# Block-selective-scan kernel: column tiles on TensorE, more states summed by DMA, skip, shift and bias by DMA, twelve product buffers, a written timetable

## The reference

```
mod = silu(c) @ wmod                                  # six rows of 512 for each sequence: sa ca ga sb cb gb
h   = layernorm(x) * (1 + ca) + sa
xs, z = split(h @ w_in.T + b_in);  z = silu(z)
dt  = softplus(xs @ w_dt.T + b_dt)
B, C = xs @ w_B.T + b_B, xs @ w_C.T + b_C             # 16 states
for each token:  state = exp(A * dt) * state + dt * B * xs;   y = sum over the 16 states of state * C
y   = ((y + D * xs) * z) @ w_out.T + b_out
x   = x + ga * (layernorm(y + h) * gamma + beta)
h   = layernorm(x) * (1 + cb) + sb
s   = h @ Win + bin                                   # 64 columns
g   = sum over 16 units of relu(s * W1 + b1) * W2 + b2
x   = x + gb * (g @ Wout + bout)
```

## Time and profile before

| | |
|---|---|
| runs | 4577.39, 4574.64, 4576.27 us |
| profiled execution | 4574.68 us |
| its span | 4572.9 us |
| granted TensorE clock, mean | 0.990 |
| busy: PE, ACT, DVE, POOL | 95%, 83%, 81%, 79% |
| DMA | 388.89 MB, mean 85 GB/s |

### The profile page before, as it was taken

One profiled execution on the slowest core, in us unless ns is written; L12 is line 12 of the kernel. 1 busy time (PEld: TensorE's weight loads), 2 busy tenths in 40 slices (PEclk: granted clock), 3 DMA queues, 4 the chain that ended last, 5 costly groups with the idle time before them and its releaser, 6 DMA issues. The chain is left out here.

```text
span 4572.9 us, 69933 instructions
## 1 busy us (share of the span) xinstructions
PE 4356.8 (95%) x22528; PEld 2784.8 (61%) x22528; DVE 3698.9 (81%) x5132; ACT 3814.2 (83%) x6371; POOL 3596.2 (79%) x1999
## 2 busy tenths in 40 slices
PE   7999999999999999999999999999999999999997
PEld 3666666666666666666666666666666666666664
DVE  3778888888888888888888888888888888888885
ACT  3788888888888888888888888888888888888885
POOL 3787878887878877877878878878788878788784
PEclk8999999999999999999999999999999999999999
DMA  4233233333233333332333333332333333333322
GB/s 138 73 79 87 81 89 82 85 81 88 80 94 81 83 88 87 85 87 77 86 93 83 89 82 84 83 90 78 91 76 89 87 86 86 86 77 89 86 77 58
DMA packets 177763, 388.89 MB, mean 85 GB/s; under 512 B 22693, under 2 KB 22693, under 8 KB 177402
## 3 DMA queue, kind: packets, MB, share of 16 engines
q1 hardware_dynamic: 140538, 250.19, 17.4%
q0 software_dynamic: 36864, 134.23, 15.3%
HBM read 215.50 MB, written 34.63 MB: 55 GB/s over the span
## 5 line engine op out<-in xcount | busy, mean ns | idle before, releaser
L379 POOL TENSOR_TENSOR work<-work,c_bc 128x1024 f32<-128x1024 f32 x1024 | 2463.3, 2418 | 765.9 <-DVE work L1140 676.7
L1140 DVE TENSOR_TENSOR_SCAN work<-work,state,b_ps 128x512 f32<-128x512 f32 x1792 | 2257.7, 1274 | 301.1 <-PE b_ps L468 272.7
L852 ACT ACTIVATE work<-u_td,b_td 128x512 f32<-128x512 f32 x2048 | 1453.2, 710 | 163.7 <-PE b_ps L468 158.3
L842 ACT ACTIVATE work<-dt_t,neg_a 128x512 f32<-128x512 f32 x2048 | 1451.3, 709 | 4.7 <-DVE work L1140 4.4
L468 PE MATMUL b_ps<-ident,work 128*128 128x128 f32 x8192 | 1253.3, 276 | 65.0 <-DVE work L1140 57.1
L468 PEld LDWEIGHTS b_ps<-ident,work 128*128 128x128 f32 x8192 | 974.8, 142 | 505.3 <-issue 303.2
L543 PEld LDWEIGHTS y_ps<-ident,work 128*128 128x128 f32 x6144 | 740.0, 142 | 481.7 <-issue 466.0
L543 PE MATMUL y_ps<-ident,work 128*128 128x128 f32 x6144 | 862.8, 273 | 1.6 <-DMA work<-work 1.3
L692 PE MATMUL dense<-h_t,w_in_t 128*128 128x512 f32 x1024 | 514.5, 599 | 1.1 <-DVE u_td L1223 1.1
L600 PE MATMUL dense<-w_out_t,proj 128*128 128x512 f32 x1024 | 509.9, 595 | 0.0
L658 PE MATMUL dense<-xs_t,w_dt_t 128*128 128x512 f32 x1024 | 501.2, 593 | 0.0
(11 more groups left out here) (115 smaller groups left out, 4530.4 us busy)
## 6 DMA issues: line engine op xcount, KB each, us to landing
c_bc<-c_d SPq DMA_DIRECT2D x512, 256.0 KB, 3.3
work<-work POOLq DMA_DIRECT2D x256, 512.0 KB, 5.6
xn<-in_x SPq DMA_DIRECT2D x128, 256.0 KB, 5.1
x<-in_x SPq DMA_DIRECT2D x128, 256.0 KB, 4.3
out_dram<-x SPq DMA_DIRECT2D x128, 256.0 KB, 4.4
work<-in_wmod SPq DMA_DIRECT2D x2, 1024.0 KB, 6.5
w_in_t<-in_w_in_t SPq DMA_DIRECT2D x2, 1024.0 KB, 9.9
gain_shift<-par_d SPq DMA_DIRECT2D x8, 256.0 KB, 6.0
```

What stands on the lines that cost most here:

```text
L379: gp.tensor_tensor(made_here, both(hs, HS_RING, s * U + i), c_bc[:, (s * N + n) % C_RING:(s * N + n) % C_RING + 1, :].to_broadcast([P, 2, ...
L842: A(decay[:, (s * U + i) % DEC_RING, :], dt_t[:, s % 2, j, :], ACT.Exp, scale=neg_a[:, j, n:n + 1]).then_inc(S["dec_done"], 1)
L852: A(v[:, n % V_RING, tb, :], u_td[:, tb, :], ACT.Copy, scale=b_td[:, s % 2, tb, n:n + 1]).then_inc(S["v_done"], 1)
L1140: V.tensor_tensor_scan(hs[:, (s * U + i) % HS_RING, :], decay[:, (s * U + i) % DEC_RING, :], b_ps[:, i % 2, :], state[:, i:i + 1] if s % N ...
```

## The change

- PE: `g` is computed in two column tiles of 64 weight columns, each with its own half of the 512 tokens (`tile_position`); `cb` in four column tiles of 32, each with 128 tokens; `turn_b` is a single transpose; `out` uses 64 rows of the array instead of 128, and its bias row is gone.
- HELD has six states: 0, 1 and 3, 4 are chains of three products (n, n + 1, n + 2), 6 and 8 begin pairs. 40 units are left for PE. A sum in a chain waits, at POOL, for the sum before it.
- The skip is a DMA from `xs_t` onto the products of state 3, the shift two DMAs of 512 KB onto `x1`, and the bias `gb * bout` one DMA of 1 MB onto `x1`; each source row of shift and bias is spread from DRAM. The POOL additions for them are gone.
- The sums are issued one product or more after the one that they wait for, in slots of their own (`sum`).
- Twelve `pr` buffers instead of ten.
- Each part has a slot written in a table (PE_AT, AT), for all engines.

```diff
--- before.py
+++ after.py
@@ -19,48 +19,75 @@
-    V_RING, DEC_RING, HS_RING, PR_RING, C_RING = 2, 6, 6, 10, 3
-    LAG = 4
-
-    HELD = (0, 6, 8, 11)
-    SUM_LAG = 3
+    V_RING, DEC_RING, HS_RING, PR_RING, C_RING = 2, 6, 6, 12, 3
+
+    HELD = (0, 1, 3, 4, 6, 8)
...
-    SKIP_AT = (8, 10)
+    SKIP_IN = 3
...
+    PE_AT = {}
+    for entry in """g.0@0 g.1@0 g.2@0 g.3@0 g.4@1 g.5@2 g.6@2 yz.0@2 g.7@3 res.0@3 yz.1@3 pre.0.0@4 yz.2@4 pre.0.1@5
...
+    AT = dict(
+        xsh=(13, 17),
+        x1=(17, 17, 19, 19),
+        bout=55,
...
+        y=(14, 14, 18, 24, 28, 28, 34, 34, 36, 37, 40, 40, 45, 46, 46, 46, 46, 46, 46, 47, 47, 51, 52, 52, 54, 54, 55, 56, 57, 61, 61, 61, 62, 62, 62, 62, 62, 64, 64, 64),
+        sum=(6, 8, 9, 11, 13, 17, 17, 20, 21, 25, 30, 32, 39, 40),
+    )
...
@@ -69,24 +96,16 @@
-    def add_slot(r):
-
-        return r + LAG + SUM_LAG * summed(r // KD) - (r in (U - 4, U - 2, U - 1)) - (r == U - 1)
-
-    ADDS = sorted((r for r in range(U) if r // KD not in HELD), key=lambda r: (add_slot(r), r))
+    SUM_AT = [i for i in range(0, U, 2) if summed(i // KD) or i // KD == SKIP_IN]
+
+    ADDS = [r for r in range(U) if r // KD not in HELD]
 
     def added(r):
 
         return ADDS.index(r) + 1
 
     def slot(*part):
...
+            def store_c(f):
+                yield AT["c_store"]
+                sp.wait_ge(S["cb_done"], at("cb_done", f, 1))
+                sp.wait_ge(S["prod_done"], at("prod_done", f - 2, U // 2))
+                for tb in range(TB):
+                    sp.dma_start(c_d[f % 2][:, tb * P:(tb + 1) * P], cb_t[tb * 2 * N:tb * 2 * N + N, :]
+                                 ).then_inc(S["c_stored"], Q)
...
@@ -379,30 +411,55 @@
                 gp.tensor_tensor(made_here, both(hs, HS_RING, s * U + i),
                                  c_bc[:, (s * N + n) % C_RING:(s * N + n) % C_RING + 1, :].to_broadcast([P, 2, T]), ALU.mult
                                  ).then_inc(S["prod_done"], 1)
-                if i in SKIP_AT:
-                    gp.wait_ge(S["prod_done"], at("prod_done", s, i // 2 + 1))
-                    gp.wait_ge(S["skip_done"], at("skip_done", s, j + 2))
-                    gp.tensor_tensor(made_here, made_here, xs_t[:, j:j + 2, :], ALU.add).then_inc(S["skip_added"], 1)
 
             def add_products(s, i):
 
                 gp.wait_ge(S["prod_done"], at("prod_done", s, i // 2 + 1))
+                if i // KD - 1 == SKIP_IN:
+                    gp.wait_ge(skip_added[i % KD // 2], (s + 1) * Q)
+                if s * SUMS + sums(i - KD):
+                    gp.wait_ge(sum_done[i % KD // 2], s * SUMS + Q * sums(i - KD))
                 gp.dma_start(both(pr, PR_RING, s * U + i), both(pr, PR_RING, s * U + i - KD), accum_op=ALU.add
                              ).then_inc(sum_done[i % KD // 2], Q)
 
+            def add_skip(s, i):
+                j = i % KD
+                gp.wait_ge(S["prod_done"], at("prod_done", s, i // 2 + 1))
+                gp.wait_ge(S["skip_done"], at("skip_done", s, j + 2))
+                gp.dma_start(both(pr, PR_RING, s * U + i), xs_t[:, j:j + 2, :], accum_op=ALU.add
+                             ).then_inc(skip_added[j // 2], Q)
+
+            def sum_up(s):
+                for i, first in zip(SUM_AT, AT["sum"]):
+                    yield first
+                    if i // KD == SKIP_IN:
+                        add_skip(s, i)
+                    if summed(i // KD):
+                        add_products(s, i)
+
+            def shifted(b):
+                for n in range(TB // 2):
+                    yield AT["xsh"][n]
+                    gp.wait_ge(S["par_stored"], 4 * Q)
+                    for tb in (2 * n, 2 * n + 1):
+                        gp.wait_ge(xb_loaded[tb], (b + 1) * Q)
+                    gp.dma_start(x1[:, 2 * n:2 * n + 2, :], par_d[1:2, b // NC:b // NC + 1, :].to_broadcast([P, 2, D]),
+                                 accum_op=ALU.add).then_inc(xsh_done[n], Q)
+
             def attended(b):
                 for tb in range(TB):
-                    yield made("out", tb) + 6
-                    if tb == 0:
-                        gp.wait_ge(S["gs_loaded"], (b // NC + 1) * 2 * Q)
-                    gp.wait_ge(xb_loaded[tb], (b + 1) * Q)
-                    gp.tensor_tensor(x1[:, tb, :], x1[:, tb, :], gs[:, 1, :], ALU.add
-                                     ).then_inc(S["xsh_done"], 1)
-                    yield made("pre", tb, 3) + 3
-                    gp.wait_ge(S["xsh_done"], at("xsh_done", b, tb + 1))
+                    yield AT["x1"][tb]
+                    gp.wait_ge(xsh_done[tb // 2], (b + 1) * Q)
                     gp.wait_ge(S["t2_done"], at("t2_done", b, tb + 1))
                     gp.tensor_tensor(x1[:, tb, :], x1[:, tb, :], tmp[:, tb, :], ALU.add
                                      ).then_inc(S["x1_done"], 1)
+
+            def add_bout(b):
+                yield AT["bout"]
+                gp.wait_ge(S["par_stored"], 4 * Q)
+                gp.wait_ge(S["xn2_done"], at("xn2_done", b, TB))
+                gp.dma_start(x1[:, :, :], par_d[3:4, b // NC:b // NC + 1, :].to_broadcast([P, TB, D]),
+                             accum_op=ALU.add).then_inc(S["bout_added"], Q)
 
             def gate_out(g):
                 yield 38
...
@@ -410,13 +467,16 @@
                 gp.wait_ge(S["late_loaded"], N_LATE * Q)
                 gp.tensor_tensor(wout_g[:, :], wout_g[:, :], wout_b[:, :], ALU.mult).then_inc(S["wout_done"], 1)
 
-            def step_size(f, b):
+            def step_size(f):
...
@@ -537,20 +595,35 @@
                 if summed(i // KD):
                     pe.wait_ge(sum_done[j // 2], s * SUMS + Q * sums(i))
                 pe.wait_ge(S["prod_done"], at("prod_done", s, i // 2 + 1))
-                if i - j % 2 in SKIP_AT:
-                    pe.wait_ge(S["skip_added"], at("skip_added", s, j // 2 + 1))
+                if i // KD == SKIP_IN:
+                    pe.wait_ge(skip_added[j // 2], (s + 1) * Q)
                 for tb in range(TB):
                     last = mm(y_ps[:, tb, j * P:(j + 1) * P], pr[:, (s * U + i) % PR_RING, tb * P:(tb + 1) * P],
                               ident[:, :], is_transpose=True, start=(i == ADDS[0]), stop=(i == ADDS[-1]))
                 last.then_inc(S["y_added"], 1)
+
+            def units(s):
+                for r, first in zip(ADDS, AT["y"]):
+                    if first < U:
+                        yield first
+                        add_unit(s, r)
+
+            def late_units(b):
+                for r, first in zip(ADDS, AT["y"]):
+                    if first >= U:
+                        yield first - U
+                        add_unit(b, r)
 
             def add_g(s, c, k):
                 if k == 0:
                     pe.wait_ge(S["w2dg_done"], 1)
                     pe.wait_ge(S["s_copied"], at("s_copied", c, 1))
                 pe.wait_ge(S["rel_done"], at("rel_done", c, k + 1))
-                mm(long(s, "g")[:, :], w2_dg[:, k, :], tmp[:, k % RELU_RING, :], start=(k == 0), stop=(k == J - 1)
-                   ).then_inc(S["g_used"], 1)
+                for h in range(2):
+                    last = mm(long(s, "g")[h * M:(h + 1) * M, 0:T // 2], w2_dg[:, k, :],
+                              tmp[:, k % RELU_RING, h * (T // 2):(h + 1) * (T // 2)], start=(k == 0), stop=(k == J - 1),
+                              tile_position=(0, h * M))
+                last.then_inc(S["g_used"], 1)
 
             def turn_y(s, b, c, j):
                 to = inside(s, "g" if j == 0 else "pre.0")
@@ -576,7 +649,9 @@
                 else:
                     pe.wait_ge(S["t1_done"], at("t1_done", b, (tb + 1) // 2))
                     pe.wait_ge(S["out_done"], at("out_done", c, tb - 1))
-                mm(to[:, :], gm[:, tb * P:(tb + 1) * P], wout_g[:, :], start=True, stop=True).then_inc(S["out_ps"], 1)
+                h = tb // 2
+                mm(to[:, :], gm[h * M:(h + 1) * M, tb % 2 * P:(tb % 2 + 1) * P], wout_g[h * M:(h + 1) * M, :], start=True,
+                   stop=True, tile_position=(h * M, 0)).then_inc(S["out_ps"], 1)
 
             def add_residual(s, b, c, tb):
                 to = long(s, "pre", tb)
@@ -663,16 +738,16 @@
             def add_cb(s, f, k):
                 if k == 0:
                     pe.wait_ge(S["vabs_done"], at("vabs_done", f, 3))
-                last = mm(long(s, "cb")[0:2 * N, :], w_cb[:, k, :], xs_t[:, k, :], start=(k == 0), stop=(k == KD - 1))
+                for tb in range(TB):
+                    last = mm(long(s, "cb")[tb * 2 * N:(tb + 1) * 2 * N, 0:P], w_cb[:, k, :],
+                              xs_t[:, k, tb * P:(tb + 1) * P], start=(k == 0), stop=(k == KD - 1),
+                              tile_position=(0, tb * 2 * N))
                 if k == KD - 1:
                     last.then_inc(S["cb_ps"], 1)
 
             def turn_b(s, f):
                 pe.wait_ge(S["cb_done"], at("cb_done", f, 1))
-                for tb in range(TB):
```

(58 more changed lines are left out.)

249 lines of the change are left out of this document (116 added, 133 removed).

## The result

| | us |
|---|---|
| after, median of 4 runs (4293.00 to 4302.81) | 4297.07 |
| before, beside it (4574.47 to 4577.39) | 4575.45 |
| ratio, 95% interval | 0.9392 [0.9376, 0.9408] |
| profiled execution after, and its span | 4302.8, 4301.1 |

The kernel is 278 us faster where 214 was forecast; 4297 lies in the range of 4240 to 4520. The mean granted clock is 0.987 (0.990 before).

The account below looks back on a forecast made before the run. PE's column stream was taken as the bound: stream 122.9 + present waits 7.8 + added waits 1.3 = 132.0 us a block against 138.7; 6.7 x 32 = 214, so 4574.7 - 214 = 4360 us, range 4240 to 4520.

Parts of the forecast that it names:

- PE's stream is the bound: PE's stream of columns sets the block's time: 130.9 of 138.7 us before, 122.9 after.
- Column tiles: On PE, tiles overlap fully: `g` 3.4 us a block instead of 6.9, `cb` 0.9 instead of 3.4.
- excursion: PE going to operands on part of the array and back: 0.22 us each, 12 a block, 2.6 us.
- The estimate from the figure of the Trainium skill: On PE, 0.79 of the ideal gain per column tile: `g` 4.3 us, `cb` 1.1 us.
- sentence on weight loads: Rival on PE: a tile's weight load can't run under the other's pass; `g` 11.7 us, time 4780 us; chance 0.05.
- What waits PE keeps: PE's waits and restarts, 7.8 us a block, grow by 1.3 with lumped additions and fuller ACT and DVE.
- the lower bound: PE's waits fall to 4.8 us a block, 3 less, as new slots fit each part more closely.
- POOL: POOL busy 110 of 132 us, not the bound; a DMA issue costs 0.96 us, at most four times that.
- DMAs: Each 0.5 MB transfer takes 2.65 us of all engines; full in slots 6 to 21, landings 7 to 10 us.
- near 34%: Sign to look for on the DMA queues: q0's share of the engines' time after the change.
- nothing is gained: Twelve product buffers give no time, as no POOL wait on `y_ps` of any size existed before.
- Rival C: At POOL's queue head, chained sums wait for landings, products and scans behind: 142.1 us a block, 4684 us; chance 0.10.

Follow-up runs that it names:

- run 10: The changed kernel with its four `cb` groups made one behind the other, where they stood at four places: 4291.2 us.
- run (4): The changed kernel with `g` and `cb` each in one column tile again and four pairs in place of two chains and two pairs: 4548.9 us.
- 3: The changed kernel without the second sums of the two chains, held states 0, 3, 6, 8 (four pairs): 4381.8 us.
- 8: The changed kernel with the skip addition done by POOL in place of the two accumulating DMAs: 4312.5 us.

## Why the prediction was right, and where it was off
- **PE's stream is the bound: right.** Each piece put back cost 67 to 92 us, 73% to 100% of its PE time, and all together added up. In the other direction it is weaker: 22 us less of PE's time in run 10 gave 6 us, inside the noise.
- **Column tiles: right, size a little off.** `g` took 4.1 us a block beside 3.4 forecast, `cb` 1.0 beside 0.9, changes 2.7 beside 2.6: cheaper than 0.22 at `g` and `cb` (0.19), dearer at `out` (0.29, which was priced as one excursion too). By these rows 64 rows of the array for `out` cost PE 1.2 us a block (4 x 0.29) and save it nothing; no run puts it back on 128. The estimate from the figure of the Trainium skill (TensorE: Matmul & The Clock Gate, Part 3), 4.3 and 1.1, was the nearer one. That part's sentence on weight loads, which would have given 11.7 us for `g`, does not hold in this trace. The stream fell by 7.1 us a block, not 8.0.
- **The step that was mis-sized: "What waits PE keeps".** I raised them by 1.3 us to 9.1. By the mean block they are 129.5 - 123.8 = 5.7 us: down 1.9 from the 7.6 of before (138.5 - 130.9), and 4.9 in the ordinary block. The 3.2 us between +1.3 and -1.9 make 102 us in 32 blocks; the stream's miss of 0.9 takes 29 back, and the start and end, longer than before, about 15. That is the 58 us by which the profiled executions gained more (272) than forecast (214). In part it is luck that the miss stayed this small: 44 of the 102 us were taken back by two other misses. I reasoned that lumps of additions and fuller neighbours would make PE wait, and that came: 42 us more waiting for the scan (1.3 a block, the very figure). But I priced at nothing the five dense waits of 0.4 to 1.4 us that were in the rows, though the lower bound named them, and they are gone. With the three stream savings undone they stay gone, and the kernel is 27 us faster than before. That run (4) holds the slots, the DMAs for skip, shift and bias and the larger ring together. The slots' own share was not isolated; the uniform rule in their place lost 434 us and more.
- **POOL: right.** Its 110.6 us are the 110 forecast. The broadcast sources cost 1.22 (shift) and 1.26 us (bias) an issue, near the low end. Other rows of POOL have to be read with care, as they overlap:
```profile
2081.11 1.22 POOL L446 DMA_DIRECT2D x<-par_d  x1 [2.03 <-DMA x<-in_x]
2081.89 2.96 POOL L454 TENSOR_TENSOR x<-x,tmp 128x512 f32<-128x512 f32 x2
```
The additions' row begins before the issue's has ended. From the end of one to the end of the other it is 2.52 us for two additions, 1.26 each, the 1.28 of before.
- **DMAs: right in size.** q0 has 38.9%, so half a MB takes 0.389 x 129.5 / 18 = 2.80 us of all engines (2.65 taken). The sign of "near 34%" was low by the prediction's own figures (47.7 of 132 us is 36%). The engines are 93% full from 2068 to 2098. In two ordinary blocks the sums land in 5.7 us (median, 9.4 at most) where it was 4.6, over the whole runs in 5.7 where it was 5.6. Between slots 6 and 21 of the ordinary block sums take 4.5 to 7.5 us, mostly less than the 7 to 10 forecast; the first shift takes 8.4 and the skip issued 0.8 us behind it 11.3.
- **The twelve buffers, "nothing is gained": wrong as a price.** I looked at waits in the kernel before, where no chain held buffers. In the changed kernel they are worth 81 us.
- **Rival C: its mechanism is real, at another place.** The sums cost POOL only 4.5 us of waiting for landings ahead of sums in the whole run, and 7.2 ahead of products. The shift is the tight place: two slots there turned a gain of 278 us into a loss of 21.

**Left open.** Why blocks differ by up to 11 us. The longest starts with POOL held 6.1 us ahead of a shift, whose load of `x` had been issued by SP 11.6 us earlier (7.8 in the ordinary block). PE then waits 3.0 and 3.7 us in that block, and for 10 us of it the granted clock is 1.2 GHz (0.78 on average from 1950 to 1960), which lengthens it further. The variants with fewer transfers in that stretch (3, 4 and 8) have even blocks. That points to the full DMA engines, but no run removed the load alone, and run 10, with all the transfers, has no block above 132.7 us either, so one such block in one profile may be chance.

## What to carry to other kernels
Work out the bound engine's column stream from starts of neighbouring groups and trust it, but take small waits that recur in each block as a term of their own when placements are rewritten. For a DMA whose result an engine adds, count what stands between issue and use in that engine's queue, and what stands behind the use on the next engine; a wait for the DMA's own source may be harmless while one slot elsewhere costs 98 us. Where a variant makes the bound engine stand still, compare its granted clock before its waits are added up. When results are held longer, price the ring that holds them in the new kernel, not in the old one.
